# Turning the context halves by transposing DMAs in a cross-attention and mixture-of-experts kernel

## The reference

```python
# attention with the context as both weight matrices (16 batches, 224 rows, 750 context rows)
h = einsum('eth,efh->etf', layernorm(x), ctx)      # 224 x 750 scores
a = gelu(h)                                        # tanh form
x = x + tanh(g_xattn) * einsum('etf,efh->eth', a, ctx)

# mixture of 8 experts over all 3584 rows, top 2
xf = layernorm(x)
scale = top-2 of softmax(xf @ gate_w), scattered to (rows, 8)
h = silu(scale*xf @ w1) * (scale*xf @ w3)
x = x + tanh(g_ffn) * sum over experts of (h @ w2)
```

## Time and profile before

| | |
|---|---|
| median of 3 runs | 914.22 us (910.63 to 915.9) |
| the profiled execution | 910.43 us, span 908.7 us |
| TensorE (PE) busy | 702.1 us, 77% of the span |
| ScalarE (ACT) busy | 469.4 us, 52% |
| VectorE (DVE) busy | 430.8 us, 47% |
| granted TensorE clock | 0.922 of full speed on average |
| first phase | about 475 us of the span |

### The profile page before, as it was taken

One profiled execution on the slowest core, in us unless ns is written; L12 is line 12 of the kernel. 1 busy time (PEld: TensorE's weight loads), 2 busy tenths in 40 slices (PEclk: granted clock), 3 DMA queues, 4 the chain that ended last, 5 costly groups with the idle time before them and its releaser, 6 DMA issues.

```text
span 908.7 us, 17157 instructions
## 1 busy us (share of the span) xinstructions
PE 702.1 (77%) x4670; PEld 472.1 (52%) x4671; DVE 430.8 (47%) x1278; ACT 469.4 (52%) x771; POOL 377.8 (42%) x470
## 2 busy tenths in 40 slices
PE   0688988779888887888885349888888887888792
PEld 0666766557666666676673324444444443444340
DVE  1256566576566675676674613333333332333230
ACT  3677777667677677667772113333333333333330
POOL 2021235444444344543545724444444444444442
PEclk9998999989899899898997559999999999999997
DMA  4225343354343434443322024555555555555454
GB/s 141 92 89 172 120 132 106 108 154 138 104 142 114 133 103 126 138 137 122 108 87 64 22 59 72 93 93 94 93 94 91 92 94 89 94 94 93 88 95 67
DMA packets 61561, 94.22 MB, mean 104 GB/s; under 512 B 15872, under 2 KB 24192, under 8 KB 61536
## 3 DMA queue, kind: packets, MB, share of 16 engines
q1 hardware_dynamic: 45136, 60.03, 21.9%
q0 software_dynamic: 16400, 33.89, 21.2%
HBM read 61.89 MB, written 32.01 MB: 103 GB/s over the span
## 4 chain that ended last, share of the span: by engine, by line
DMA 47%; issue 14%; PE 13%; DVE 8%; ACT 7%; POOL 5%; SPq 3%; DVEq 1%; POOLq 0%; ACTq 0%
DMA out_rows<-ctx_raw,meta 33%; DMA ctx_raw<-in_ctx 11%; PE bank L1112 7%; SPq L386 3%; PE bank L1100 2%; DMA w_raw<-in_L_ffn_w 2%; POOL route_table L463 2%; PE bank L1086 2%; PE bank L1057 2%; ACT ctx_part L579 2%; DVE ctx_part L773 2%; ACT squares L545 1%; ACT ctxT L584 1%; ACT w2s L613 1%; DVE a_part L782 1%
## 5 line engine op out<-in xcount | busy, mean ns | idle before, releaser
L1241 PE MATMUL bank<-w,ctxT 128*128 x756 | 176.7, 384 | 0.1
L1112 PE MATMUL bank<-ctx_part,a_part 125*112 125x512 f16 x576 | 156.1, 423 | 12.3 <-DVE a_part L782 12.3
L516 POOL DMA_INDIRECT out_rows<-ctx_raw,meta x63 | 99.8, 1585 | 149.1 <-DMA out_rows<-ctx_raw,meta 132.8
L1100 PE MATMUL bank<-xnT,ctxT 128*125 128x224 f16 x1152 | 126.9, 270 | 8.4 <-DVE xnT L803 8.4
L1100 PEld LDWEIGHTS bank<-xnT,ctxT 128*125 128x125 f16 x1152 | 118.3, 144 | 9.3 <-issue 8.6
L1241 PEld LDWEIGHTS bank<-w,ctxT 128*128 128x128 f16 x756 | 74.8, 99 | 78.0 <-issue 4.7
L1112 PEld LDWEIGHTS bank<-ctx_part,a_part 125*112 125x112 f16 x576 | 79.8, 144 | 61.6 <-issue 16.2
L584 ACT ACTIVATE ctxT<-bank 128x1000 f16<-128x1000 f16 x96 | 94.6, 1006 | 28.5 <-PE bank L1057 28.5
L1221 PE MATMUL bank<-ident,ctx_raw 128*128 128x128 f32 x256 | 42.8, 291 | 69.8 <-DMA ctx_raw<-xf_rows,meta 69.4
L1251 PE MATMUL bank<-w2s,ctxT 128*128 x378 | 91.9, 379 | 1.4 <-DVE ctxT L1017 1.3
L507 POOL DMA_INDIRECT ctx_raw<-xf_rows,meta x66 | 64.6, 978 | 64.4 <-issue 45.0
(11 more groups left out here) (131 smaller groups left out, 1040.7 us busy)
## 6 DMA issues: line engine op xcount, KB each, us to landing
ctx_raw<-in_ctx SPq DMA_DIRECT2D x48, 500.0 KB
w_raw<-in_L_ffn_w SPq DMA_DIRECT2D x24, 512.0 KB, 5.7
x<-in_x SPq DMA_DIRECT2D x16, 448.0 KB, 4.9
out_rows<-x SPq DMA_DIRECT2D x16, 448.0 KB, 3.3
xf_rows<-xf SPq DMA_DIRECT2D x16, 448.0 KB, 7.9
meta<-route_table SPq DMA_DIRECT2D x66, 1.0 KB, 1.7
ctx_raw<-xf_rows,meta POOLq DMA_INDIRECT x66, 3.7
route_table<-route,pos_i POOLq DMA_INDIRECT x64, 4.5
```

The costliest lines, as they stand in the source:

```text
L516: g.indirect_dma_start(out=out, out_offset=bass.IndirectOffsetOnAxis(ap=meta[n][:, 0:1], axis=0), in_=y_sb[n % 2], in_offset=None, compute ...
L1100: ins = t_.matmul(dst, ctxT[u][:, hc * KD + k, c * CS:c * CS + CR], xnT[u][:, hx, k, :], start=j == 0, stop=j == KD * len(PARTS) - 1)
L1112: ins = t_.matmul(O_ps[t][0:TT, :], a_part[ha][:, c, t * TT:(t + 1) * TT], ctx_part[u][hc][:, c, :], start=c == 0 and (ha, hc) == PARTS[0] ...
L1241: ins = t_.matmul(H_ps[u][:, :], rows, w, start=m == 0, stop=m == KD * len(PARTS) - 1)
```

## The change

The 48 transposes and six copies of each batch go. In their place SyncE issues, once a batch, two transposing DMAs (`turn_ctx`): each takes one whole half, `ctx_part[u][h]`, 128 partitions of 6 x 512 fp16 numbers (768 KB), and writes it as 24 blocks of 128 x 128 into `ctxT[u]`. Both are issued after the store of the normed rows and ahead of `load_ctx(i + 2)` for q = 2: the one of the high halves when all high halves of batch i + 1 are written, the one of the low halves when all low halves are. `scores` waits for both.

The chunks become 128 rows, five whole ones and a last one of `CL` = 110. The rows of the last chunk above 110 are set to zero once, ahead of the first load. The third load of a batch becomes two transfers, of 128 and of 110 rows. The totals of the squares no longer share a PSUM bank with transposed blocks, so the waits and the second place that kept them apart (`late_total`, `total_taken`, `late_tot_out`) go too. The fp16 identity goes.

```diff
-CR, NC = 125, 6
+CR, NC = P, 6
+CL = C - (NC - 1) * CR
...
-        ctx_part = [[sb(f"ctx_part{u}{h}", [CR, NC, D], F16) for h in range(2)] for u in range(2)]
-        ctxT_buf = [sb(f"ctxT{u}", [P, 2 * KD * NC * CS], F16) for u in range(2)]
+        ctx_part = [[sb(f"ctx_part{u}{h}", [P, NC, D], F16) for h in range(2)] for u in range(2)]
+        ctxT_buf = [sb(f"ctxT{u}", [P, 2 * NC * KD * CR], F16) for u in range(2)]
...
+                if q < NQ - 1:
+                    sp.dma_start(ctx_raw[:, 2 * q:2 * q + 2, :],
+                                 ctx[bass.ds(i * C + 2 * q * CR, 2 * CR), :].rearrange("(c p) d -> p c d", p=CR)).then_inc(ctx_loaded[q], 16)
+                else:
+                    sp.dma_start(ctx_raw[:, 2 * q, :], ctx[bass.ds(i * C + 2 * q * CR, CR), :]).then_inc(ctx_loaded[q], 16)
+                    sp.dma_start(ctx_raw[0:CL, 2 * q + 1, :], ctx[bass.ds(i * C + (2 * q + 1) * CR, CL), :]).then_inc(ctx_loaded[q], 16)
+
+            def turn_ctx(i, u):
+
+                for h, split in enumerate((ctx_high, ctx_split)):
+                    hold(sp, split, i * NQ + NQ)
+                    sp.dma_start_transpose(ctxT[u][:, h, :, :], ctx_part[u][h][:, :, :].rearrange("p c d -> p (c d)")).then_inc(ctxT_ready[u], 16)
...
                 if later(i, 1):
                     store_norm(i - 1)
+                if not last:
+                    turn_ctx(i + 1, w)
                 if load_two:
-                    sp.wait_ge(ctx_split, i * NQ + 2 * NQ)
                     load_ctx(i + 2, NQ - 1)
...
-            def ctxT_out(i, u, c):
-
-                act.wait_ge(ctxT_made, i * NC + c + 1)
-                a.activation(ctxT[u][:, :, c * CS:c * CS + CR], T_half[c % 2], ACT.Copy).then_inc(ctxT_ready, 1)
...
+            v.memset(ctx_raw[96:P, NC - 1, :], 0.0).then_inc(pad_made, 1)
...
-            def trans_ctx(i, u, c):
-
-                n = i * NC + c
-                pe.wait_ge(ctx_split, i * NQ + c // 2 + 1)
-                if later(i, 1) or c >= 2:
-                    pe.wait_ge(ctxT_ready, n - 1)
-                if c == 0:
-                    pe.wait_ge(ctx_gsum_ready, i + 1)
-                for h in range(2):
-                    for k in range(KD):
-                        ins = t_.transpose(T_half[c % 2][:, h * KD + k, :], ctx_part[u][h][:, c, k * P:(k + 1) * P], ident16[0:CR, 0:CR])
-                ins.then_inc(ctxT_made, 1)
...
-                pe.wait_ge(ctxT_ready, i * NC + 2 * q + 2)
+                pe.wait_ge(ctxT_ready[u], h * 32 + 32)
```

More of the change, by code:

```diff
@@ L45 @@
 TT = S // 2
-CR, NC = 125, 6
+CR, NC = P, 6
+CL = C - (NC - 1) * CR
 NQ = NC // 2
-CS = CR + 1
 KD = D // P
@@ L130, in build @@
         ctx_raw = sb("ctx_raw", [P, NC, D])
-        ctx_part = [[sb(f"ctx_part{u}{h}", [CR, NC, D], F16) for h in range(2)] for u in range(2)]
-        ctxT_buf = [sb(f"ctxT{u}", [P, 2 * KD * NC * CS], F16) for u in range(2)]
-        ctxT = [b[:, :].rearrange("p (g c) -> p g c", g=2 * KD) for b in ctxT_buf]
+        ctx_part = [[sb(f"ctx_part{u}{h}", [P, NC, D], F16) for h in range(2)] for u in range(2)]
+        ctxT_buf = [sb(f"ctxT{u}", [P, 2 * NC * KD * CR], F16) for u in range(2)]
+        ctxT = [b[:, :].rearrange("p (h g c) -> p h g c", h=2, g=NC * KD) for b in ctxT_buf]
         squares = [sb(f"squares{n}", [P, KD * HID], F16) for n in range(2)]
@@ L200, in build @@
         T_ps, H_ps, O_ps, X_ps, L_ps = bank[0:2], bank[2:4], bank[4:6], bank[6], bank[7]
-        T_half = [t[:, :].bitcast(F16)[:, 0:2 * KD * CS].rearrange("p (g c) -> p g c", g=2 * KD)[:, :, 0:CR] for t in T_ps]
-        spare = KD * CS
-        ctx_tot, w_tot = T_ps[0][:, spare:spare + NQ], [t[:, spare + NQ:spare + NQ + 1] for t in T_ps]
+        ctx_tot, w_tot = T_ps[0][:, 0:NQ], T_ps[1][:, 0:1]
         lg_ps, rk_ps = L_ps[0:TT, 0:2 * E], L_ps[0:TT, 64:64 + 2 * E]
@@ L221, in build @@
         w_high, w_split, cols_ready = (sem(n) for n in ("w_high", "w_split", "cols_ready"))
-        ctxT_made, ctxT_ready = sem("ctxT_made"), sem("ctxT_ready")
+        pad_made = sem("pad_made")
+        ctxT_ready = [sem(f"ctxT_ready{u}") for u in range(2)]
         h_made, a_ready, attn_part = sem("h_made"), sem("a_ready"), sem("attn_part")
@@ L316, in _ @@
             for q in range(NQ):
+                if q == NQ - 1:
+                    sp.wait_ge(pad_made, 1)
                 load_ctx(0, q)
@@ L328, in _ @@
                 sp.wait_ge(ctx_split, q + 1)
+                if q == NQ - 1:
+                    turn_ctx(0, 0)
                 load_ctx(1, q)
@@ L344, in step @@
                 last = isinstance(i, int) and i == B - 1
+                w = 1 - u
                 if later(i, 1):
@@ L626, in _ @@
             ctx_high_part(0, 0, 2)
-            ctxT_out(0, 0, 0)
             xnT_high(1, 0, 1)
-            ctxT_out(0, 0, 1)
-            for c in range(2, NC):
-                ctxT_out(0, 0, c)
             act.wait_ge(table_ready, 48)
@@ L664, in step @@
                 if not last:
-                    ctxT_out(i + 1, w, 2)
-                if not last:
                     xnT_high(i * 4 + 2, w, 0)
@@ L671, in step @@
                     first_matrix(weight_squares, i, u, h)
-                if not last:
-                    ctxT_out(i + 1, w, 3)
                 if two:
@@ L1087, in small_trans, with scores @@
                 ins.then_inc(small_made, 1)
-            def scores(i, u, q):
+            def scores(i, u, h, q):
                 n, m = i * NQ + q, (u + q) % 2
@@ L1099, in scores @@
                     for j, (k, (hc, hx)) in enumerate((k, part) for k in range(KD) for part in PARTS):
-                        ins = t_.matmul(dst, ctxT[u][:, hc * KD + k, c * CS:c * CS + CR], xnT[u][:, hx, k, :], start=j == 0, stop=j == KD * len(PARTS) - 1)
+                        ins = t_.matmul(dst, ctxT[u][:, hc, c * KD + k, :], xnT[u][:, hx, k, :], start=j == 0, stop=j == KD * len(PARTS) - 1)
                 ins.then_inc(h_made, 1)
@@ L1148, in _ @@
                 rows_norm1(0, t, t)
-                trans_ctx(0, 0, t)
-            for c in range(2, NC):
-                trans_ctx(0, 0, c)
             pe.wait_ge(pool_seq, POOL_START)
@@ L1157, in step @@
                 w = 1 - u
-                scores(i, u, 0)
+                scores(i, u, h, 0)
                 if not last:
                     ctx_total(i + 1)
-                late_matrix(late_total, i, u, h)
-                scores(i, u, 1)
+                late_matrix(weight_total, i, u, h)
+                scores(i, u, h, 1)
                 if later(i, 2):
@@ L1165, in step @@
                 attend(i, u, 0)
-                if not last:
-                    late_matrix(total_taken, i, u, h)
-                    trans_ctx(i + 1, w, 0)
-                    trans_ctx(i + 1, w, 1)
-                scores(i, u, 2)
+                scores(i, u, h, 2)
                 if later(i, 1):
@@ L1177, in step @@
                     rows_norm2(i - 1, i * 4 + 1, 1)
-                if not last:
-                    trans_ctx(i + 1, w, 2)
                 if u:
                     first_matrix(weight_total, i, u, h)
-                if not last:
-                    trans_ctx(i + 1, w, 3)
                 if not last:
@@ L1189, in step @@
                 attend(i, u, 2, (1,))
-                if not last:
-                    trans_ctx(i + 1, w, 4)
                 if not u:
                     first_matrix(weight_total, i, u, h)
-                if not last:
-                    trans_ctx(i + 1, w, 5)
                 if later(i, 2) and not last:
@@ L1283 @@
 POOL_STEPS = 21
-POOL_IDENT = 6
-POOL_START = 17
+POOL_IDENT = 5
+POOL_START = 16
 _INS = ['x', 'ctx_1024', 'g_xattn', 'g_ffn', 'L0_ffn_gate_w', 'L0_ffn_w1', 'L0_ffn_w2', 'L0_ffn_w3']
```

35 lines of the change are left out of this document (8 added, 27 removed).

## The result

The changed kernel took 941.47 us (median of 4, 939.05 to 946.68) against 914.65 us (median of 4, 910.63 to 915.9): 1.031 of the time before, 95% interval 1.027 to 1.035. I had forecast 870 us, faster. It is 3.1% slower.

A forecast was written before the change was run, and what follows sets the result against it. Two nearly equal rings, not TensorE, bound the kernel. Six pairs -32, batches 13 to 15 -4, start -9, second batch's wait -1, together -46, then +3 unplaced: 914 - 43 = 871, said 870 us; range 845 to 1080.

The forecast's parts named there:

- two rings: First phase: load, squares, scale, halves, next load; beside it scores, total, scale, halves, scores; nearly equal, 59.1 us a batch pair.
- the five engines behind the slow loads: Context loads: 125 rows use five of sixteen DMA engines, so the third load takes 11.67 us; 128 rows use all 16.
- the pair if turning were hidden: First phase, two successive batches: 53.0 us against 59.1 if turning and load come early enough.
- the 9 forecast: Start of the kernel: faster first loads save 8.5 us, turning batch 0 adds 4.5, a 4.83 us TensorE wait goes; net -9.
- the cut: Point in each batch where the third low half of the next batch's context is done; forecast times count from it.
- The start, -1.2 forecast: First turning DMA, behind the store of the normed rows: starts about 1.2 us before the cut.
- The packets, 2 x 3.4 forecast: Two turning DMAs a batch: 192 packets of 18 ns to an engine, 3.4 us a half, through at +5.6 us.
- only for the microsecond or two of issue: SyncE queue: store of x and other loads wait behind the turnings only this long; SyncE held would prove the prediction wrong.
- The landing: End of the turning: landed about 1.5 us after the engines are through, at +7 us after the cut.
- a cold clock as a rival of its own: TensorE, with less work: granted clock falls from 0.91 to 0.80, 43 us lost in 15 batches, about 910 us; chance 0.05.
- my own formula: T is us per turned half; 4T - 17.2 = 46 / 7.5 sets loss against the 46 us gain, break-even T = 5.8.
- T of 5 to 6.5: Case of slower turning, T in us per half; T = 5.2 to 6.5 gives 895 to 935 us; chance 0.10.

The follow-up runs named there:

- the split loads: Kernel before, TensorE still turning the context, with each context load cut into 112 and 13 rows: 875.03 us against 903.12, ratio 0.969.

## Why the prediction was wrong

**Right:** what bounds the kernel (two rings, and not TensorE at 77%); the five engines behind the slow loads, with 3.2 us a pair for it alone; the pair if turning were hidden, 53.0 forecast and 51.3 measured; 192 packets of 18 ns in the median for each engine and half; the second phase untouched. The start gave 6.0 us of the 9 forecast. That clock, ScalarE or loads would be the cause is refuted by the kernel without turning.

**The step that failed** is "both are through the engines at -1.2 + 2 x 3.4 = +5.6 us after the cut and landed about 1.5 us later ... +7 ... so turning is just hidden". It landed at +13.3, and every term was short (medians from the fourth batch on):

- *The start, -1.2 forecast, +0.3 measured.* The issue came at -2.1, earlier than forecast, but I let the first packets go at the issue, and they came 2.5 us after it. 1.5 us. In batch 0, where no store stands ahead, they came after 1.3.
- *The packets, 2 x 3.4 forecast, 4.9 + 4.0 measured.* The median of 18 ns was right and the mean of 25.8 is what counts; at the start, with little beside, a half takes 3.8 to 4.0. The last packet is through at +9.4 instead of +5.6. 2.2 us.
- *SyncE "only for the microsecond or two of issue".* It is held 10 us a batch. The low half could be issued only at +4.0 for that. This did not delay the second turning's packets much (they start 0.2 us behind those of the first), but the third context load goes out at +8.1 and every store and load behind it likewise. I had named this as what would prove me wrong, and gave it no price and no chance. Nothing in the trace of before bounds it: every transfer there is plain. No run changes the hold alone, so its own price stays open.
- *The landing.* 1.5 us forecast after the last packet; 0.5 to 0.6 measured without scatters near, 3.9 with them (6.2 in the batch shown). 2.4 us. Taking them out lowers the pair by 4.7 us more than in the kernel before, and moving them by 4.5 to 7.1. By that it is the largest term of the loss, and I had no rival for it, though the scatters and their place in GpSimd's order stood in the trace of before.

Then the clock: the wait leaves TensorE cold, and the first scores step of a batch is 1.9 us longer in the batches shown, over the six pairs 8.1 us a pair instead of 5.5. Not all of it shows: from scores to cut a pair takes 38.0 us instead of 36.9. I had a cold clock as a rival of its own, by less work; it came as a follower of the wait. One reading of the prediction was also wrong, and nothing hangs on it: the prediction puts the load of 110 rows on 10 engines, where the largest divisor up to 16, the rule it used for 125 rows, is 11.

Seen through my own formula, 941 us answers to T = 6.6 us a half (4T - 17.2 = (27 + 43) / 7.5), above the break-even of 5.8 and just past the case to which I gave 0.10, "T of 5 to 6.5". The packets alone are T = 4.5, on the winning side of it; start, hold and landing did the rest. The bare rate was not the error: the Trainium skill (Advanced Engine Details and Errata, "X-Bar Transpose (TRN2)") expects 350 to 400 GB/s and the runs show about 215 with little beside, near the 18 ns that I took; and its 1309 ns for one block (VectorE: DVE Perf Modes, "The three transpose paths") does not add up over blocks, since 24 of them went through in 3.8 us.

**Left open.** Why a transfer whose last packet is through needs up to 6 us more to signal beside the scatters; only that it hangs on their overlap in time is shown. What of the 10 us of holding is work of SyncE and what is waiting for room is not told apart; in batch 0 each half holds it for 3.6 to 3.9 us, and from the fourth batch on, behind other transfers, a high half for 5.7 to 7.1, or up to 10.5 behind loads on five engines, so part of it hangs on what stands ahead. Why a low half issued by itself starts later, the runs don't show either. Turning the high half by DMA and the low one by TensorE was not tried; by the runs above it could gain over the split loads at most 0.7 us a pair (55.5 - 54.8), before the cost of the low half, and that is less than single executions tell apart; by whole times, 0.973 against 0.969, it would gain nothing.

## What to carry to other kernels

Price a new kind of DMA by three terms, the issue that holds its queue, the time to the first packet, and the landing after the last, and not by its bytes alone; if the trace of before has no such transfer, these are what the range must hold. An operation that moves off a busy engine gains only what that engine had on the path: here 4.2 us a pair, against 12.9 for its replacement. And look for the small side effect in the diff: 125 rows became 128, and that part alone, made by splitting each load into 112 and 13 rows, was worth 3.1%.

## What the runs showed of the hardware

- A transposing DMA of 768 KB held the issuing SyncE 3.6 to 7.1 us (median 3.9), a plain one 0.3 to 0.5; 10 to 11 us for 1.5 MB in two pieces or six. With loads on five engines ahead of it, the most was 10.5.
- Its packets ran at about 215 GB/s with little beside, where plain loads ran at 348.
- With scatters of GpSimd in flight, the second transposing DMA of a batch landed 1.2 to 6.2 us behind its last packet (median 3.9); without them, 0.5 to 1.4, in most batches 0.5.
- A weight load of 128 columns took 98 ns in the scores, one of 125 columns 137 (medians of 1152 each); the matmuls were the same, 260 and 259 ns, so that it gained nothing here.
